# One wait for a batch of row gathers, in place of one for each half of the batch, in a two-layer graph network kernel

## What is computed

```python
def _ngcf_conv(x, W1, W2, src, dst, n_nodes):
    deg_out = clip(segment_sum(ones, src), 1.0)
    deg_in = clip(segment_sum(ones, dst), 1.0)
    norm = rsqrt(deg_out[src] * deg_in[dst])
    h_src, h_dst = x[src], x[dst]
    msg = (h_src @ W1 + h_src * h_dst @ W2) * norm[:, None]
    return x @ W1 + segment_sum(msg, dst)

h = relu(_ngcf_conv(x, W1_1, W2_1, ...))
h = _ngcf_conv(h, W1_2, W2_2, ...)
out = layernorm(x + h)
```

## Time and profile before

| | us |
|---|---|
| median of 3 timed runs | 1456.77 |
| lowest and highest of them | 1445.62, 1461.82 |
| the profiled execution's own time | 1438.36 |
| its span in the trace | 1436.8 |

### The profile page before, as it was taken

The page is one execution under the profiler, slowest core; times in us unless marked ns, Lnnn a source line. Parts: engine busy times, 40 slices in busy tenths (PEclk is TensorE's granted clock), DMA queues, the critical chain, the costliest instruction groups (busy, mean ns, idle before and its releaser), DMA issues. The chain is left out here.

```text
span 1436.8 us, 33831 instructions
## 1 busy us (share of the span) xinstructions
PE 970.4 (68%) x13162; PEld 878.0 (61%) x13162; DVE 978.3 (68%) x2390; ACT 737.9 (51%) x2763; POOL 800.0 (56%) x813
## 2 busy tenths in 40 slices
PE   1676466667776677766873566777777777776676
PEld 1575345666666666665872456666666666765575
DVE  7577567665666665666882256868677877677687
ACT  3112135555556555656881245545645556465565
POOL 7475545666665566665205665656556656555640
PEclk9999677887777777877995577878787878778877
DMA  9955111222222222222212122333333233323332
GB/s 209 187 198 204 20 18 47 56 55 47 51 54 54 55 54 50 47 54 53 53 67 72 33 59 62 76 75 74 76 73 75 61 74 75 73 60 75 77 66 56
DMA packets 148692, 105.09 MB, mean 73 GB/s; under 512 B 115768, under 2 KB 128760, under 8 KB 147836
## 3 DMA queue, kind: packets, MB, share of 16 engines
q1 hardware_dynamic: 123176, 71.17, 18.4%
q0 software_dynamic: 25216, 32.50, 12.1%
q10 hardware_dynamic: 212, 0.42, 0.1%
HBM read 58.92 MB, written 45.11 MB: 72 GB/s over the span
## 5 line engine op out<-in xcount | busy, mean ns | idle before, releaser
L849 POOL DMA_INDIRECT c_rows<-table,k_row_i x394 | 379.9, 964 | 322.6 <-PE c_sum L882 122.2
L849 POOL DMA_INDIRECT k_rows<-table,k_row_i x346 | 338.8, 979 | 240.4 <-PE c_sum L882 112.7
L882 PE MATMUL c_sum<-c_rows,c_sel 128*128 128x64 bf16 x4701 | 254.5, 221 | 196.3 <-issue 174.7
L882 PEld LDWEIGHTS c_sum<-c_rows,c_sel 128*128 128x128 bf16 x4701 | 224.9, 116 | 227.8 <-issue 220.7
L990 ACT ACTIVATE c_uvt<-c_turn 128x512 f32<-128x512 f32 (+1 forms) x198 | 106.9, 591 | 476.1 <-remote 427.8
L1205 DVE TENSOR_TENSOR c_sum<-c_sum,c_own 128x512 f32<-128x512 f32 (+1 forms) x96 | 66.7, 694 | 279.1 <-remote 268.8
L882 PE MATMUL c_sum<-c_lo,c_sel 128*128 128x64 bf16 x1567 | 219.8, 218 | 48.9 <-issue 48.4
L882 PE MATMUL c_sum<-c_yr,c_sel 128*128 128x64 bf16 x1567 | 219.3, 217 | 44.1 <-issue 40.8
L882 PE MATMUL c_sum<-c_rest,c_sel 128*128 128x64 bf16 x1567 | 218.6, 218 | 43.5 <-issue 43.5
L1146 DVE TENSOR_SCALAR c_sel<-k_place,k_grid 128x512 bf16<-128x512 f16 (+1 forms) x788 | 239.2, 372 | 0.0
L882 PEld LDWEIGHTS c_sum<-c_yr,c_sel 128*128 128x128 bf16 x1567 | 175.4, 115 | 63.0 <-issue 59.8
(11 more groups left out here) (210 smaller groups left out, 1234.0 us busy)
## 6 DMA issues: line engine op xcount, KB each, us to landing
table<-c_y SPq DMA_DIRECT2D x47, 384.0 KB
out<-c_y SPq DMA_DIRECT2D x47, 256.0 KB
c_res<-in_x SPq DMA_DIRECT2D x46, 256.0 KB
table<-k_xh SPq DMA_DIRECT2D x4, 1820.0 KB
c_rows<-table,k_row_i POOLq DMA_INDIRECT x394
k_rows<-table,k_row_i POOLq DMA_INDIRECT x346
table<-k_xh SPq DMA_DIRECT2D x1, 3575.0 KB
table<-k_xh SPq DMA_DIRECT2D x1, 1040.0 KB
```

What stands on the lines that cost most here:

```text
L849: nc.gpsimd.indirect_dma_start(out=rows[:, b % RING, i], out_offset=None, in_=tables[l], in_offset=bass.IndirectOffsetOnAxis(ap=k.row_i[:, ...
L882: last = nc.tensor.matmul(p_sum[g % BANKS][:, t - GROUP[g][0], :], sel[:, b % 2, i, n * P:(n + 1) * P], part[:, i], start=first and q == 0 ...
```

## The change

The first gather of a batch now waits for the full sum of the batch that had its place, and no other gather of the batch waits. Nothing is issued in another order on any engine.

```diff
             for b in range((BEGUN, 0)[l], BATCHES):
                 for i in range(BATCH[b]):
                     c = FIRST[b] + i
-                    if i % HALF_BATCH == 0:
-                        done(pool, summed, sums_of(b - RING) - 1 + i // HALF_BATCH)
+                    if i == 0:
+                        done(pool, summed, sums_of(b - RING))
                     nc.gpsimd.indirect_dma_start(out=rows[:, b % RING, i], out_offset=None, in_=tables[l],
```

## The result

| | before | after |
|---|---|---|
| median of the timed runs, us | 1452.59 (4 runs) | 1600.01 (4 runs) |
| lowest and highest | 1445.62, 1461.82 | 1599.8, 1606.33 |
| span of the profiled execution | 1436.8 | 1598.5 |
| mean granted clock of PE | 0.798 | 0.757 |

The changed kernel is slower: the ratio is 1.102, with a 95% interval from 1.095 to 1.110. The direction and the mechanism of the forecast held; its size, +45 us (1502 on 1456.77) against +147, did not, and the result lies outside the range.

The account below looks back on a forecast made before the run. The prediction took the batch period as POOL's gathers, PE's release after them and PE's remaining work. Terms 26 + 20 + 8 = 54 us on 1438.36 gave 1492, or 1511 from the median; it took 1502, range 1448 to 1538.

Parts of the forecast that it names:

- Rows ready in time, cost 0: Gathers starting at the full sum end 10.3 us later, rows are wanted some 27 us later; cost 0.
- A run of gathers holds PE, and a pause frees it: POOL's gathers nearly stop PE and its signals after a while; PE is free 1.0 to 1.5 us after the last.
- Rival 1: No change: PE's gaps are not owed to gathers, or the hold is by time and work fits; 1457 us, chance 0.20.
- One eight costs 0.9 us a batch in layer 1 and 0.75 in layer 0: Extra period of eight gathers in one run over two fours with a pause; 26 us in layer 1, 20 in layer 0.
- the eights of before: Batches before the change whose eight gathers ran without middle pause: 15 periods in layer 1, 8 in layer 0.
- 128 less 85 are left for after the release: If PE is held by instruction count, 85 of a batch's 128 matmuls pass during the run, the rest after it.
- Only 29 and 26 batches pay: Only periods then in two fours lengthen: 29 of 44 in layer 1, 26 of 34 in layer 0.
- Look-up steps, 8 us: Layer 0, batches 8 to 12: a longer hold of DVE's pick delays look-ups, 1.6 us a batch; bounds 0 to 32.
- Ends, −3 to 3: Starts and ends of the layers: later first and last waits leave PE less to do behind them; cost 0.
- Rival 2: Faster: one release of PE a batch instead of two, period 12.3 us against 12.8; 1417 us, chance 0.08.
- Rival 3: Much slower: late signals in a run of eight make DVE, then PE, late; 1546 us, chance 0.06.

Follow-up runs that it names:

- fours_later: Against the kernel before: first four gathers wait for the full sum, the next four for the next batch's first half sum; 1445.66 us, ratio 0.995.
- eight_at_half: Against the kernel before: one run of eight gathers a batch, released by the first half sum of the next batch; 1598.98 us, ratio 1.099.
- five_and_three: Against the kernel before: PE's first signal after its third chunk; five gathers go at the full sum, three at that signal; 1387.60 us, ratio 0.965.
- six_and_two: Against the kernel before: PE's first signal after its third chunk; six gathers go at the full sum, two at that signal; 1388.91 us, ratio 0.963.
- pause_long: Changed kernel plus a 512-column POOL memset between fourth and fifth gather, a gap of 0.81 us; 1524.24 us, ratio 1.060 against the kernel before.
- pause_longer: Changed kernel plus three 512-column POOL memsets between fourth and fifth gather, a gap of 1.98 us; 1415.19 us, ratio 0.983 against the kernel before.

## Why the prediction was wrong in size

- **Rows ready in time, cost 0**: right. The splits wait as before, and fours_later, later still, is no slower.
- **A run of gathers holds PE, and a pause frees it**: right, and it is the whole effect. Rival 1, which the Trainium skill's sentence that PE never waits on another engine supports ("SBUF — State Buffer", "Who interferes with whom"), is out: equal work took 1600 us in runs of eight and 1389 in runs of six and two. Whether it is a port that holds PE the runs don't tell, so the Trainium skill is contradicted in its conclusion ("PE and ACT never wait on anyone") and not in what it says of the ports.
- **One eight costs 0.9 us a batch in layer 1 and 0.75 in layer 0**: this is the step that failed. A run of eight in every batch cost 1.99 us a batch in layer 1 and 2.14 in layer 0. The step took the eights of before as what an eight costs. They were a selection, and their periods, 13.0 to 13.7, are no measure of a kernel in which every run is an eight: there the means are 14.4 to 15.2.
- **"128 less 85 are left for after the release"**: the same error as a count. In the changed kernel the hold looks like a matter of count and not of time, as the text preferred, but the count is smaller: in layer 0, 54 to 59 matmuls at once in a settled run, whether they took 3.7 us or 5.2, and over all its runs of eight 62.9 in the mean from a run's start to 1 us past its end, not 85. So 65 of 128 are left, not 43. It is no constant of all kernels, though: in eight_at_half the first burst is anything from 33 to 82.
- **Only 29 and 26 batches pay**: wrong. All 34 periods of layer 0 grew and 43 of the 44 of layer 1 (all but its first), those that had been eights too, since 13.68 became 15.16. With 78 periods at 2.06 us the two terms are 160 us where 46 stood.
- **Look-up steps, 8 us**: measured 1.8, within the bounds given. **Ends, −3 to 3**: layer 1's first wait cost 2.7 and its end gave 4.3 back; the first wait of layer 0, for which no sum was made, cost 6.8, and layer 0's end with the stretch between the layers gave 6.6 back. Together they are 1.4 us less, within the bounds, but by terms larger than the bounds that happen to cancel.
- **Rival 2** had the right terms for the period, 0.26 + 10.05 + 1.5, and put 0.5 for the sums left over. With the 3.0 that they took, the same sum gives 14.8. The trace of before held a warning: in its steady stretches the first fours of a batch let 63.8 matmuls through in the mean and the eights 86.4. One fixed count gives not both, so the eights were of another kind than the fours.
- **Rival 3** (DVE late behind late signals): not seen. PE's gaps are "issue", and L1156 and L1241 hardly hold it (18.8 and 6.9 us in the whole span, 20.7 and 9.4 before).

How many matmuls PE starts from a run's start to 1 us past its end, over both layers (runs set apart by more than 0.9 us; for the eights of before only those of the steady stretches):

| gathers in the run, kernel | length, us | matmuls, mean |
|---|---|---|
| 3, five_and_three | 3.5 | 57.4 |
| 4, before | 4.7 | 49.2 |
| 5, five_and_three | 6.1 | 52.6 |
| 6, six_and_two | 7.4 | 59.7 |
| 8, after | 10.0 | 62.9 |
| 8, eight_at_half | 10.0 | 69.6 |
| 8, before | 10.2 | 86.4 |
| 8 with a gap of 0.81, pause_long | 10.6 | 82.2 |

From four gathers to eight the time doubles, and what gets through grows by 28% in the changed kernel (41% in eight_at_half), singles included. The row of the fours is a mean of two kinds: in the steady stretches the first fours of a batch, behind a gap of 2.1 us (median), let 63.8 through, and the second fours, behind the middle pause of 1.2 us, only 36.9. In pause_longer the fours behind its 1.98 us let 64.4 through. So a longer pause gives PE more than its own length, which may be why that kernel is faster than before; no run took this apart. And the eights of before don't fit a fixed count. What in PE's path is counted, and why an indexed gather stops it, stays open: no view shows it, and none of the runs took it apart. One candidate, that PE waits for its instructions to be loaded, has nothing for it in the trace: in the hold of the changed kernel from 1080.9 to 1092.6 the DMA queues that the profile calls "instruction" (q8 and q14) moved no packet.

## What to carry to other kernels

Where an engine shows idle time with "issue" as its cause beside another engine's gathers, count what it gets through from a run's start to its release; if that number grows far less than the run, the loss is near one hold a run, and the length of the runs and what is owed behind them are to be tuned, not the waits. A wait that costs nothing by the waits' view can be worth 147 us for the pause that it makes. And a pattern that a kernel falls into only sometimes is a selection by its own cause: its rows don't price the kernel in which it is forced.

## What the runs showed of the hardware

- While POOL issues indirect gathers (0.94 us each, 0.30 between them), PE gets some 50 to 70 matmuls on (means of 49 to 70 for runs of three to eight, but 86 for the eights of before), the last of them a few at a time, some 0.7 or 1.4 us apart, and is free mostly 0.9 to 1.8 us behind the last gather.
- Plain loads issued by POOL, 0.55 us each, with as many packets, hold nothing: 384 sums in 35 us, and the granted clock is at 1.00 (2.4 GHz).
- A pause in the middle of eight gathers gives nothing that can be told at 0.40 us, 4 points of the ratio at 0.81 (1.060 against 1.102) and 12 at 1.98 (0.983), with nothing but POOL's own memset in it. Where the run ahead was only three gathers, a gap of 0.69 to 0.89 was enough for the next run to let 50 matmuls through.
